# One block for scans and experts: an expert block woven in every four scan tiles

## The reference

```
xn  = layernorm(x)                                # x: 2 x 2048 x 256
# scan over time, for each of 256 channels and 16 states
delta = softplus(xn @ W_delta.T + bias)
Bs, Cs = xn @ W_B.T, xn @ W_C.T                   # 256*16 columns each
a_bar = exp(delta * A)
h = a_bar * h + (a_bar - 1) / A * Bs * xn         # along the 2048 tokens of a row
y = sum over the 16 states of h * Cs
# experts: top 2 of 8 for each token
h1 = gelu(xn @ W1[e] + b1[e])                     # 256 -> 1024
y2 = h1 @ W2[e] + b2[e]                           # 1024 -> 256
out = x + y + sum over 2 experts of weight * y2
```

## Time and profile before

| | |
|---|---|
| time, median of 3 runs | 1458.48 us (1458.33 to 1459.33) |
| span of the profiled execution | 1459.1 us |
| PE busy | 1220.7 us (84%) |
| DVE busy | 1122.0 us (77%) |
| POOL busy | 870.4 us (60%) |
| ACT busy | 593.4 us (41%) |
| mean DMA rate | 130 GB/s |

### The profile page before, as it was taken

How to read it: one execution, slowest core, us unless ns; L and a number is a source line. 1 busy time by engine, 2 the same in 40 slices (tenths; PEclk the granted TensorE clock), 3 DMA queues, 4 the chain that set the end, 5 groups by cost and what they waited for, 6 DMA issues and landing times. The chain is left out here.

```text
span 1459.1 us, 23731 instructions
## 1 busy us (share of the span) xinstructions
PE 1220.7 (84%) x7674; PEld 727.2 (50%) x7674; DVE 1122.0 (77%) x1357; ACT 593.4 (41%) x1128; POOL 870.4 (60%) x582
## 2 busy tenths in 40 slices
PE   1668888878879776999999999999888878888775
PEld 0533333333333324899989999995333333333332
DVE  6869999999999995334334334336999999999998
ACT  3735425425434533444444444443532532532331
POOL 3639979979988983010010010015978978988975
PEclk9569999999999998999999999999999999999998
DMA  6672312321321325777777777762102101101100
GB/s 208 220 243 80 133 70 83 112 93 53 137 97 47 112 101 182 257 244 256 257 243 258 257 243 258 257 200 89 40 15 61 36 18 58 40 18 54 37 11 30
DMA packets 89546, 189.84 MB, mean 130 GB/s; under 512 B 13249, under 2 KB 63937, under 8 KB 79521
## 3 DMA queue, kind: packets, MB, share of 16 engines
q1 hardware_dynamic: 75872, 126.56, 26.2%
q0 software_dynamic: 13632, 62.80, 13.2%
HBM read 139.52 MB, written 49.81 MB: 130 GB/s over the span
## 5 line engine op out<-in xcount | busy, mean ns | idle before, releaser
L783 POOL TENSOR_TENSOR uxb<-ub,x 128x512 f32<-128x512 f32 x256 | 466.9, 1825 | 100.3 <-DVE ub L861 97.1
L934 PE MATMUL bank<-k_xT,k_WC 128*128 (+1 forms) x1536 | 388.2, 390 | 150.8 <-DVE hcb L878 130.3
L869 DVE TENSOR_TENSOR_SCAN hb<-aexp,state,uxb 128x512 f32<-128x512 f32 x256 | 417.0, 1629 | 25.4 <-POOL uxb L783 25.4
L934 PE MATMUL bank<-k_xT,k_WB 128*128 (+1 forms) x1536 | 388.2, 391 | 10.3 <-DVEq L849 10.0
L934 PEld LDWEIGHTS bank<-k_xT,k_WC 128*128 128x128 f16 x1536 | 139.1, 99 | 382.8 <-DVE hcb L878 207.0
L691 ACT ACTIVATE state<-hb 128x1 f32<-128x1 f32 x256 | 51.7, 202 | 553.7 <-DVE hb L869 553.7
L934 PEld LDWEIGHTS bank<-k_xT,k_WB 128*128 128x128 f16 x1536 | 153.9, 101 | 203.7 <-issue 21.4
L1062 POOL DMA_DIRECT2D w<-wsplit x39 | 20.9, 537 | 381.0 <-DVE yo L1192 372.5
L1102 PE MATMUL bank<-xbt,k_xT 128*128 128x256 f16 x1872 | 213.0, 274 | 2.7 <-ACT xbt L1148 2.7
L1117 PE MATMUL bank<-w,hs 128*128 128x256 f16 x1872 | 210.6, 273 | 0.0
L1102 PEld LDWEIGHTS bank<-xbt,k_xT 128*128 128x128 f16 x1872 | 184.2, 98 | 25.4 <-issue 1.8
(11 more groups left out here) (121 smaller groups left out, 759.3 us busy)
## 6 DMA issues: line engine op xcount, KB each, us to landing
k_xT<-wsplit SPq DMA_DIRECT2D x39, 1024.0 KB, 4.9
w<-wsplit POOLq DMA_DIRECT2D x39, 1024.0 KB, 5.4
k_yall<-in_W SPq DMA_DIRECT2D x32, 512.0 KB, 4.3
wsplit<-k_yall SPq DMA_DIRECT2D x32, 512.0 KB, 3.2
xs<-k_yall SPq DMA_DIRECT2D x1, 9984.0 KB, 32.1
k_yall<-xs SPq DMA_DIRECT2D x39, 256.0 KB, 4.8
ys<-yo SPq DMA_DIRECT2D x39, 256.0 KB, 2.2
b<-in_b POOLq DMA_DIRECT2D x39, 128.0 KB, 5.4
```

Of the source, the lines that this page charges most:

```text
L783: nc.gpsimd.tensor_tensor(uxb[:, s % 2], ub[:, s % 2], x32[:, hf], ALU.mult).then_inc(ux_done, 1)
L869: v.tensor_tensor_scan(hb[:, s % AR], aexp[:, s % AR], uxb[:, s % 2], state[:, s:s + 1], ALU.mult, ALU.add).then_inc(h_done, 1)
L934: ins = mm(bank[:], W[:, a, kc, n, hf * P:(hf + 1) * P], chunk(xT, c)[:, b, kc, :], start=(k == 1), stop=(k == 3 * KC))
```

## The change

`scan_phase` and `expert_phase` are replaced by one function, `scan_and_experts`, in which every engine's program is written out over a running tile number g from 0 to 255 (`TILE_N`). What each engine does at tile g:

- Scan tile: ScalarE makes `aexp` five tiles ahead (ring of 6) and with one more activation `em1 = aexp - 1` (`less_one`, four tiles ahead, ring of 2). GpSimd makes `ax = em1 * x` (`times_x`, ring of 2). VectorE multiplies by B in place in PSUM (`ux_op`), and the scan reads `aexp` from SBUF and its other input from PSUM. The sum of y is kept in SBUF (`ysum`).
- The 32 weight pieces are split one every two tiles: ScalarE scales piece k at g = 2k and rounds it at g = 2k+1, GpSimd subtracts at g = 2k+3 (`low_piece`). One scatter at each of the first 64 tiles.
- Experts: with E0 = 74 and b0 = E0 + 4b, block b has its hidden layer on TensorE and its gelus on ScalarE at tile b0, the turn of block b+1 at b0+1, the second layer of block b-1 at b0+2; VectorE casts (`high_h`) at b0+2, ScalarE takes the turned slots of block b+1 at b0+2, GpSimd subtracts for the low part (`low_h`, on VectorE before) at b0+3. The hidden layer has two PSUM banks where it had four. `w1`, `w2` and `h32` have one buffer.
- The turned slots, the second layer, z and the turned rows of y all share one PSUM bank (`Sps`). Each use waits until the use before it has been taken out (`shared_made`, `shared_taken`, order by `shared_bank_uses`).
- From tile F0 = 233 on, eight gathers in three tiles on GpSimd; VectorE weighs and adds the experts' rows (`add_expert`, 64 of 128x256). Rows with x and y added go through DRAM (`mid`) in between.

```diff
-    AR = 4
+    AR, ER, XR, HR, BR, CR = 6, 2, 2, 3, 3, 2
+    LEAD = AR - 1
...
+    Bps, Cps, Hps, Sps = banks[0:3], banks[3:5], banks[5:7], banks[7]
...
+        def less_one(g):
+            act.wait_ge(a_ready, g + 1)
+            if g >= ER:
+                act.wait_ge(ax_done, g - ER + 1)
+            nc.scalar.activation(em1[:, g % ER], aexp[:, g % AR], ACT.Copy, bias=-1.0).then_inc(em1_done, 1)
...
+        def take_x(b):
+            act.wait_ge(shared_made, USE["turn", b] + 1)
+            if b >= 1:
+                act.wait_ge(H_done, b * PAIRS)
+            nc.scalar.activation(xbt.rearrange("p a c s -> p (a c s)"), Sps[:].bitcast(F16),
+                                 ACT.Copy).then_inc(shared_taken, 1)
...
+        for g in range(TILE_N):
+            c, s = divmod(g, TILES)
+            if g + LEAD < TILE_N:
+                exp_tile(g + LEAD)
+            if g + LEAD - 1 < TILE_N:
+                less_one(g + LEAD - 1)
+            if g >= 1 and (g - 1) // TILES % RCH != RCH - 1:
+                save_state(g - 1)
+            if g < 2 * SPLITS:
+                if g % 2 == 0:
+                    scale_piece(g // 2)
+                else:
+                    high_piece(g // 2)
...
+            if g >= 1 and turn_block(g - 1) is not None:
+                take_x(turn_block(g - 1))
+            b = block_at(g, 0)
+            if b is not None:
+                gelus(b)
...
+        def times_x(g):
+            c, hf, n = tile(g)
+            pool.wait_ge(em1_done, g + 1)
+            if g >= XR:
+                pool.wait_ge(ux_done, g - XR + 1)
...
+            nc.gpsimd.tensor_tensor(ax[:, g % XR], em1[:, g % ER], x32[:, hf], ALU.mult).then_inc(ax_done, 1)
...
+        def low_piece(k):
+            par = k % 2
+            pool.wait_ge(p_hi, k + 1)
...
+        def low_h(b, q):
+            fs = slice(q * (FC // 2), (q + 1) * (FC // 2))
+            pool.wait_ge(hi_done, b * 2 + q + 1)
+            nc.gpsimd.tensor_tensor(hs[b % 2][:, 1, fs, :], h32[:, fs, :], hs[b % 2][:, 0, fs, :],
+                                    ALU.subtract).then_inc(lo_done, 1)
...
+        for g in range(TILE_N):
+            c, s = divmod(g, TILES)
+            times_x(g)
...
+            if g >= 3 and g % 2 == 1 and (g - 3) // 2 < SPLITS:
+                low_piece((g - 3) // 2)
+            if g < 2 * NT:
+                i, k = g // 2, g % 2
+                nc.gpsimd.indirect_dma_start(
...
+            b = block_at(g, 3)
+            if b is not None:
+                for q in range(2):
+                    low_h(b, q)
...
+        def ux_op(g):
+            bank = Bps[g % BR][:]
+            dve.wait_ge(ax_done, g + 1)
+            dve.wait_ge(B_ready, g + 1)
+            v.tensor_tensor(bank, ax[:, g % XR], bank, ALU.mult).then_inc(ux_done, 1)
...
+        for g in range(TILE_N):
+            c, s = divmod(g, TILES)
+            if g >= 1 and down_block(g - 1) is not None:
+                take_y(down_block(g - 1))
+            if block_at(g, 2) is not None:
+                for q in range(2):
+                    high_h(block_at(g, 2), q)
+            if g >= 1 and row_part(g - 1) is not None:
+                add_rows(*row_part(g - 1))
+            if g + 1 < TILE_N:
+                ux_op(g + 1)
+            scan_op(g)
+            if g >= 1:
+                acc_op(g - 1)
+            hc_op(g)
...
+        def project_b(g):
+            if g >= BR:
+                pe.wait_ge(h_done, g - BR + 1)
+            project(Bps[g % BR], WB, g, B_ready)
+
+        def project_c(g):
+            if g >= CR:
+                pe.wait_ge(c_taken, g - CR + 1)
...
+        def shared_free(use):
+            if USE[use] >= 1:
+                pe.wait_ge(shared_taken, USE[use])
...
+        def hidden(b):
+            pe.wait_ge(shared_taken, USE["turn", b] + 1)
+            pe.wait_ge(w1_in, (b + 1) * 32)
             for fc in range(FC):
+                if fc % 2 == 0 and (b or fc >= 4):
+
+                    pe.wait_ge(gelu_done, b * FC + fc - 2)
...
+        def down(b):
+            pe.wait_ge(w2_in, (b + 1) * 32)
+            pe.wait_ge(lo_done, b * 2 + 2)
+            shared_free(("down", b))
...
+        project_b(0)
+        for g in range(TILE_N):
+            if g + 1 < TILE_N:
+                project_b(g + 1)
+            project_c(g)
+            if block_at(g, 0) is not None:
+                hidden(block_at(g, 0))
+            if turn_block(g) is not None:
+                turn(turn_block(g))
+            if down_block(g) is not None:
+                down(down_block(g))
+            if row_part(g) is not None:
+                turn_rows(*row_part(g))
+            if z_part(g) is not None:
+                project_z(*z_part(g))
```

More of the change, by code:

```diff
@@ L514, in scan_phase, with block_at, turn_block, down_block @@
-def scan_phase(nc, io, keep, banks, ctx, row):
-    split_weights, combine = row == 0, row == 1
+TILE_N = NCH * TILES
+E0 = 74
+STEP = 4
+F0 = E0 + STEP * NBLK + 3
+SPLITS = E * NPIECE
+def block_at(g, shift):
+    b, r = divmod(g - E0 - shift, STEP)
+    return b if r == 0 and 0 <= b < NBLK else None
+def turn_block(g):
+    return 0 if g == E0 - 1 else block_at(g, 1 - STEP) if g > E0 else None
+def down_block(g):
+    return block_at(g, 2 + STEP)
+def z_part(g):
+    c, s = divmod(g, TILES)
+    return (c + 1, (s - 13) // 4) if s in (13, 17) and c + 1 < NCH else None
@@ new lines, in row_part, with shared_bank_uses @@
+def row_part(g):
+    c, s = divmod(g, TILES)
+    return (c - 1, (s - 5) // 4) if s in (5, 9) and c >= 1 else None
+def shared_bank_uses():
+    order = []
+    for g in range(TILE_N):
+        if turn_block(g) is not None:
+            order.append(("turn", turn_block(g)))
+        if down_block(g) is not None:
+            order.append(("down", down_block(g)))
+        if row_part(g) is not None:
+            order.append(("row",) + row_part(g))
+        if z_part(g) is not None:
+            order.append(("z",) + z_part(g))
+    order += [("row", NCH - 1, 0), ("row", NCH - 1, 1)]
+    return {name: i for i, name in enumerate(order)}
@@ L590, in scan_phase @@
[L590 to L616, removed]
@@ L632, in _ @@
     def _(sp):
[L633 to L679, removed]
+        def load_piece(k):
+            ex, pc, par = k // NPIECE, k % NPIECE, k % 2
+            if k >= 2:
+                sp.wait_ge(p_lo, k - 1)
+            if pc < KC:
+                sp.dma_start(wst[:, par, :], io["W1"][ex, pc * P:(pc + 1) * P, :]).then_inc(piece_in[par], 16)
+            else:
+                fc = (pc - KC) * (FC // 2)
+                sp.dma_start(wst[:, par, :].rearrange("p (c d) -> p c d", d=D),
+                             io["W2"][ex, fc * P:(fc + FC // 2) * P, :].rearrange("(c p) d -> p c d", p=P))\
+                    .then_inc(piece_in[par], 16)
@@ L693, in exp_tile @@
[L693 to L695 removed]
+        def exp_tile(g):
+            c, hf, n = tile(g)
             if n == 0:
[L698 to L701 removed]
+                act.wait_ge(delta_done, c * KC + hf if c else hf)
+            if g >= AR:
+                act.wait_ge(h_done, g - AR + 1)
+            nc.scalar.activation(aexp[:, g % AR], dcur[:, hf, :], ACT.Exp,
@@ new lines, in _ @@
+        act.wait_ge(keep["zeros_out"], 16)
+        for g in range(LEAD):
+            exp_tile(g)
+        for g in range(LEAD - 1):
+            less_one(g)
+        for g in range(TILE_N):
+            c, s = divmod(g, TILES)
+            if g + LEAD < TILE_N:
[7 more added lines that the diff above has]
+                    scale_piece(g // 2)
+                else:
+                    high_piece(g // 2)
+            if g >= 1 and z_part(g - 1) is not None:
+                take_z(*z_part(g - 1))
+                if z_part(g - 1)[1] == KC - 1:
+                    softplus(c + 1)
+            if g >= 1 and turn_block(g - 1) is not None:
[3 more added lines that the diff above has]
+                gelus(b)
@@ L846, in _ @@
+        for g in range(TILE_N, F0 + 3 * NCH):
+            part = finish_part(g)
+            for j in range(part[1] * 3, min(part[1] * 3 + 3, 2 * CT)):
+                gather(part[0], j)
     @block.vector
@@ new lines, in hc_op @@
+        def hc_op(g):
+            c, hf, n = tile(g)
+            bank = Cps[g % CR][:]
+            dve.wait_ge(C_ready, g + 1)
+            dve.wait_ge(h_done, g + 1)
+            if n == 0 and c >= 2:
+                dve.wait_ge(shared_made, USE["row", c - 2, 1] + 1)
+            dst, done = (ysum[:, c % 2, hf], c_taken) if n == 0 else (bank, hc_done)
+            v.scalar_tensor_tensor(dst, hb[:, g % HR], keep["rA"][:, hf, n:n + 1], bank, ALU.mult,
+                                   ALU.mult).then_inc(done, 1)
@@ L902, in body @@
-        def body(c, last, final):
-            for s in range(1, TILES + 1):
-                if not (final and s == TILES):
-                    u_op(c, s)
-                scan_op(c, s - 1)
-                if s >= 2:
-                    acc_op(c, s - 2)
```

(66 more changed lines are left out.)

770 lines of the change are left out of this document (316 added, 454 removed).

## The result

The changed kernel takes 1862.41 us, median of 4 runs (1858.5 to 1863.86), against 1458.5 us before: ratio 1.2756, 95% interval 1.2738 to 1.2774. The forecast was 1840 us. The profiled execution has a span of 1859.4 us.

The account below looks back on a forecast made before the run. The prediction took queue waits between GpSimd and ScalarE, and TensorE's resulting idling before down, to bound the changed kernel: prologue 97.9 + tiles 0 to 73 344 + expert tiles 1276 + end 121 = 1839, forecast 1840 us, range 1740 to 1905.

Parts of the forecast that it names:

- the tail: Tiles 234 to 255 and the end: gathers on GpSimd at 4.6 us a tile set the pace, 121 us.
- The wait at the pieces: Tiles 0 to 73: GpSimd's low_piece waits 1.9 us for ScalarE's high_piece, queued behind less_one, at each of 32 pieces.
- The hold before down: Expert blocks: down waits for take_x through casts, low_h, times_x, less_one and save_state; TensorE idles 7.1 us, 37 times.
- The clock behind the hold: Expert blocks: after some 7 us idle TensorE returns at a lower clock, costing 2.3 us more a block.
- The gelu stall: Hidden layer: its third pair waits for two gelus delayed by a table load, 1.3 us a block.
- The block: Tiles 74 to 233: a block woven into four tiles has a period of 32.1 us, against 25.6 before.
- What falls in once a chunk: Expert stretch: two turns of y, z and a gelu stall longer by the softplus, 6.2 us, five times.
- the expected gain: Four tiles and a block: 25.6 us before; woven together they need 21.3 us of TensorE.
- No such queue on ScalarE: Rival: em1's ring of two does not hold ScalarE, both waits fall, block 22.5 us, total 1424; chance 0.07.
- The hold absent, the wait at the pieces not: Rival: no hold before down, but GpSimd still waits at the weight pieces; 1485 us, still slower; chance 0.05.

Follow-up runs that it names:

- run 1: Changed kernel with four buffers for em1 in place of two; 1461.51 us, ratio to before 1.0009.
- run 3: Changed kernel with only low_piece moved one tile later on GpSimd; 1795.36 us, ratio to before 1.2299.
- run 5: Changed kernel with take_x first in ScalarE's tile and low_piece one tile later, em1 still two buffers; 1442.27 us, ratio to before 0.988.
- run 2: Changed kernel with only take_x moved to the front of ScalarE's tile, ahead of the exponential and less_one; 1507.19 us, ratio to before 1.0318.
- run 4: Changed kernel with low_h moved back from GpSimd to VectorE, behind each cast; 1525.85 us, ratio to before 1.0448.
- run 6: On top of run 5, ScalarE does a one-column gelu before waiting for the hidden layer, to load the table early; 1405.28 us, ratio to before 0.9632.
- run 7: On top of run 6, three buffers for the gathered rows in place of two; 1373.26 us, ratio to before 0.9413.

## Why the prediction was right, and where it was off

**By stretch.** At the borders that the forecast used (tile 74's first group at 438.6, the end of tile 233's last projection at 1707.1) it said 97.9, 344, 1276 and 121 us, and 97.5, 341.1, 1268.5 and 152.3 were measured. The forecast is within 8 us in each of the first three and 31 short in the last. The total came nearer than the tail alone would have it, since the first three were together 11 us too long. Two of the sums were also rounded up: 29.7 + 2.3 is 32.0 for a block, not 32.1, and the terms of the tail add up to 120, not 121; that is 5 us in all.

**The wait at the pieces**: said 1.9 us, 32 times; measured 1.84 in the row above, and 2.1 in the mean, since a piece behind a softplus waits up to 7.4 us, which the forecast booked as 14 us on the side. The stretch was to lose 61 us without it; it lost 61 in run 1, 65 in run 3, and 69 in run 5, which moved `take_x` as well. TensorE's clock fell there to 0.88 in the mean, and the loss that I put at 0 to 10 us and took at 0 can't be seen in the sum.

**The hold before down**: said 7.1 us, 37 times; measured 7.2. The links differ a little: the two `low_h` took 4.58 us in place of 4.26. The first runs beside the second cast, and its longest instances are 2.5 us where 2.13 is clean. The Trainium skill, "GPSIMD Engine Reference", Specifications, names contention of GpSimd with VectorE instructions in a two-port mode; that the cast runs in one no row here says, but beside it `low_h` is 0.3 us longer, once a block. That the hold is this chain is shown by runs 1, 2 and 4, each of which takes out another link.

**The clock behind the hold**: said 2.3 us. The `down` matmuls are busy 286.0 us in all; less 2 x 5.4 for the two that nothing holds, that is 7.44 us each for 37, so 2.0 us lost. With full clock in runs 1 and 5 the loss is gone, without a change to any matmul.

**The gelu stall**: said 1.3 us, measured 1.1 from start to start, of which 0.95 are idle by the profile. Run 6 removed it in 34 of 39 blocks and won 37.0 us. On the drain that the Trainium skill, "ScalarE: Activation LUTs", What ACT_TABLE_LOAD costs, adds to a table load, the measurement decides against the page: with it the stall would have been 2.7 us, and in run 6 the next activation starts 0.02 us behind the load.

**The block** was to last 32.1 us. Where no z, softplus or turn of y falls into it, three blocks in a row last 31.4, 32.7 and 31.7 us, 31.9 in the mean, from the starts of these `down` and the next at 1170.41; the longest has the slowest matmuls:

```profile
1074.65 6.88 PE L1133 MATMUL bank<-k_x 128*128 128x256 f16 x48 [7.18 <-ACT stage L829]
1106.03 8.22 PE L1133 MATMUL bank<-k_x,k_xT 128*128 128x256 f16 x48 [7.19 <-ACT stage L829]
1138.75 7.25 PE L1133 MATMUL bank<-k_x 128*128 128x256 f16 x48 [7.18 <-ACT stage L829]
```

What falls in once a chunk was priced at 6.2 us and is some 4.8: a turn of y takes 0.44 us where 1.0 was put, and the softplus lengthens the gelu stall by 1.3 where 1.6 was put. The 36 periods from the first `down` on last 1170.8 us in all, 16 less than by the forecast's terms; the two ends of the stretch last 8 more, which I did not trace.

**The step that was mis-sized** is the tail: "it has 8 gathers and 3 products in three tiles", taken at 4.6 us a tile. That priced the work of the queue and left out its wait: a gather into one of two buffers waits until VectorE has added the rows of two chunks before, and these additions stand at the end of VectorE's tile. It cost six waits, 33.6 us, and run 7 took 32.0 us off the time with a third buffer. The gathers themselves were nearly as priced, 0.97 us in the mean and 0.16 to 0.31 before most of them. The same kind of dependence that made the forecast for the first two stretches was overlooked in the third.

**Where the expected gain is.** Run 1 has no hold and is as slow as the kernel before. Before, the two scan blocks with the end of the kernel were 924.9 us, 3.61 a tile. Its 925 us for the experts and about 158 tiles stand against 436.3 + 158 x 3.61 = 1007, a gain of 82. The rest loses it again: the first 75 tiles take 284 us where 75 x 3.61 is 271, and the last 23 take 155 us where 23 x 3.61 is 83. The first 64 tiles carry a scatter each and a piece in every second one, the last 23 all 64 gathers. Of this loss, run 5 takes back 8 us in the first (276 us, by the two orders) and run 7 some 30 in the last (125 us, by the third buffer); that the rest comes from the packed side work is argued and not shown. The block itself came near the 21.3 us that the forecast gave TensorE for it only in run 6, where one without z, softplus or turn lasts 21.5.

**The rivals.** "No such queue on ScalarE" was given 1424 us; run 5, the kernel without both holds, took 1442. "The hold absent, the wait at the pieces not" was given 1485 and run 2 took 1507. These are 18 and 22 us short, as the forecast itself was 22 short of 1862: the 31 us of the tail are in all three, and the other stretches give some of them back. So the prices of the two holds were right, and the same term is missing everywhere.

## What to carry to other kernels

When several stages are woven into one order, add up the work of each engine, but then follow each ring to the instruction that frees it, and ask what stands behind the instruction that waits for it: here ScalarE, only 40% busy, waited in `less_one` for a buffer that GpSimd would free two tiles later, and the copy that TensorE needed stood behind it in the queue. The two holds of this kind cost 400 us. A short wait for something harmless placed ahead of a time-critical instruction is repaired by one more buffer or by the order alone. Do the same count at the ends of the kernel, where the side work is packed densest.

## What the runs showed of the hardware

TensorE's clock makes a wait cost more than its length. In two blocks with a wait of 7.2 us the mean granted clock was 0.89 and 0.84 of full, between its two levels of 1.2 and 2.4 GHz:

```profile
900.00:931.60 31.60, 23.46 (x158) 15.54 (x157) 14.54 (x21) 11.95 (x24) 9.57 (x6) 0.89 0.26 87
931.60:963.20 31.60, 23.47 (x152) 15.54 (x151) 14.09 (x20) 10.74 (x23) 9.56 (x6) 0.84 0.29 101
```

The 48 matmuls behind the wait took 6.81 and 8.04 us there in place of 5.4, and 7.44 in the mean of 37, so a hold of 7.2 us cost 9.2. Where the holds were gone the clock was 1.00 over 911 us.

The scan with one input in PSUM takes 1.27 us, as with both in SBUF and undisturbed. None of the 256 takes more than 1.28 us, though 202 of them overlap with products or indirect DMAs of GpSimd. The gathers, 0.98 to 1.96 us before, took 0.95 to 1.20 us in the changed kernel, whose scans no longer read two inputs from SBUF; no run separates that from what else changed around them.
